# First two chunks of a linear-attention and gated-FFN block: one group of weight maxima less, a weight cast shared by two engines, other small moves, and the last output in two parts

## The chip, the cores and the metric

One core of one Trainium2 chip. The metric is the device time of one execution in microseconds (us); of several executions the median is given. TensorE is called PE (its weight loads PEld), VectorE DVE, ScalarE ACT, GpSimd POOL and SyncE SP. PEq, DVEq, ACTq, POOLq and SPq are the queues from which an engine issues register loads and DMAs.

## The reference

The input x is 8 x 1024 tokens of 256 channels, in float32. With xn = layernorm(x) the output is x + attention(xn) + ffn(xn):

```
q = elu(xn @ Wq.T) + 1;  k = elu(xn @ Wk.T) + 1;  v = xn @ Wv.T         (16 heads of 16)
attn = (q @ (k.T v)) / max(q @ sum(k), 1e-6)                           (per head, over 1024 tokens)
local = xn[t-1]*conv_w[:,0] + xn[t]*conv_w[:,1] + xn[t+1]*conv_w[:,2] + conv_b
attention = (attn + local) @ Wp.T + bp
ffn = (silu(xn @ wg.T) * (xn @ wu.T)) @ wd.T                           (768 hidden, int32 weights / 127)
```

## The kernel before

The kernel works through 16 chunks of 512 tokens, two (c = 0, 1) to each of the 8 batches b. Weights are brought in once. To multiply in float16 without losing float32's precision, each operand is the sum of a high part (suffix `h`) and a low part (`l`), and a product takes three matmuls (high x high, low x high, high x low). The integer weights of gate, up and down (g, u, d) need no low part if they are small; a flag that is read into a register (`TENSOR_LOAD`, then a branch) tells that. A power of two that scales a weight into float16's range comes from the maximum of that weight over all its elements.

Such a maximum is made in stages. DVE reduces each weight along its rows (`weight_maximum`, L665). For a **group** of weights (`GROUPS`) PE transposes the column of maxima (`turn_maxima`, L1056), DVE takes the maximum of each row (L647) and puts it on a diagonal (L649, together `across`), PE multiplies by ones so that every partition has it (`spread_maxima`, L1063), and DVE makes the powers and scales of it (`powers`, L656 to L661, four short steps, each waiting for the one before). The groups are [k, v, q], [g, u], [d] and [conv_w, conv_b, p], numbered 0 to 3. Group 3 gives the scales of the convolution's taps (`attention_scales`), group 2 that of d (`down_scales`).

A chunk's step on PE is: k and v (`project_kv(0)`, `(1)`), q, accumulation of k.T v, six blocks of gate and up (`gate_up(0)` to `(5)`, 8 matmuls of 512 columns each), and the down projection in two halves (`down(0)`, `down(1)`, 24 matmuls of 256 columns each). `gate_up(j)` from j = 2 on waits for `hid` of block j - 2, since it takes that block's PSUM banks. On ACT a block is silu (`act_g`, L536) and the high part of the hidden values (`hh`, L544); on DVE it is the product (`hid`, L896) and the low part (`hl`, L902). `down(0)` waits for `hid` of block 4, then for each `hh` and `hl`.

Every engine has a program written out by hand: its `step` function lists the work in the order in which the engine does it, and semaphores hold engines together. Nothing is reordered at run time, so an instruction that waits holds all that stand behind it on its engine. The first chunk (`not past`) is special: the scales are made in between, and k and v of this chunk are multiplied in float32 straight from the raw weights (`project_first`, L1085). In the second chunk (b = 0, c = 1) the float16 weights of k and v are used for the first time: `project_kv` waits for `k_hi`, `v_hi` and, at its last third, for `kv_lo` (both low parts, `kv_wl`, L677). Chunks from b = 1 on attend to the batch before as well.

What the prediction's steps touch in the first chunk:

- DVE: v's high part (L709), `gate_up_scales`, g's high part (L684), the statistics of the next chunk's layernorm (`stats`), d's maximum, then `hid` and `hl` mixed with `across(2)`, `down_scales` and the late maxima of p, conv_w and conv_b; at its end `across(3)`, `attention_scales` (with `cb`, L764, and `cw`, L768), the two `kv_wl` and the two residual sums (`put_res`, L912).
- ACT: u's high part (`u_wh`, L455), table load, silu and `hh` of each block, the next chunk's `xn_h` (`x_high`, L444), d's high part (`d_wh`, L455) behind silu of block 3, and q's exponential at the end.
- POOL: k's high part (L393), k's sum (`k_sb`, L397), the normalised tokens (L326), their low part (`xn_l`, L408), the issue of two DMAs that add x to the bias in `xb` (L323), the transposed tokens `xT` (L361), and q's sum (`q_sb`, L416).
- SP: all other loads, the two transposing DMAs of `xn_h` and `xn_l`, and the stores.

At the end DVE writes the last 256 tokens of the output in one instruction (`output`, L823) and SP stores them in one DMA (`store_pair`).

## Time and profile before

| | |
|---|---|
| median of 3 runs | 507.55 us (507.19 to 507.74) |
| profiled execution, its own time | 506.9 us |
| its span in the profile | 505.3 us |
| PE busy | 491.4 us, 97% |
| PEld busy | 306.1 us, 61% |
| DVE busy | 430.5 us, 85% |
| ACT busy | 334.3 us, 66% |
| POOL busy | 144.7 us, 29% |
| chain that ended last | PE 88%, DVE 5%, ACT 3%, DMA 2% |
| granted PE clock | 0.999 of full speed |

The time is some 1.6 us longer than the span, which begins and ends with the first and last recorded instruction. The profiled execution lies 0.65 us below the median. The page's slices (12.6 us each) show PE at 7, 8, 8, 8 tenths in the first four slices, at 9 in all others but the last, which is at 7. A timeline row gives the start in us, the duration in us, engine, line and operation, output and inputs, and in square brackets the idle time before it and what ended it; several like instructions in a row share one line, whose duration runs from the first start to the last end.

### The profile page before, as it was taken

How to read it: one execution, taken by the hardware profiler on the slowest of the kernel's cores; microseconds unless marked ns; L12 is line 12 of the kernel's file. 1: busy time of each engine (PE TensorE's matmuls, PEld its weight loads, DVE VectorE, ACT ScalarE, POOL GpSimd, SP SyncE). 2: the span in 40 equal slices, each digit the busy share in tenths (PEclk: the TensorE clock that was granted, in tenths of full speed). 3: DMA queues.
4: the chain of work that ended last, by engine and by line, in shares of the span. 5: the costliest groups of instructions: out<-in, count | busy, mean ns of one | idle time of the engine just before them, and what ended most of it. 6: DMA issues, size and time to landing. Idle time of an engine off the chain costs nothing.

```text
span 505.3 us, 11017 instructions
## 1 busy us (share of the span) xinstructions
PE 491.4 (97%) x3968; PEld 306.1 (61%) x3968; DVE 430.5 (85%) x833; ACT 334.3 (66%) x522; POOL 144.7 (29%) x152
## 2 busy tenths in 40 slices
PE   7888999999999999999999999999999999999997
PEld 6545364755747566474756657475565756657576
DVE  4889898889888898988889888889888889897786
ACT  2676866667485775757667485667758576674770
...
DMA packets 68653, 45.36 MB, mean 90 GB/s; under 512 B 33424, under 2 KB 68112, under 8 KB 68624
## 3 DMA queue, kind: packets, MB, share of 16 engines
...
q14 instruction: 10, 0.08, 0.0%
...
## 4 chain that ended last, share of the span: by engine, by line
PE 88%; DVE 5%; ACT 3%; DMA 2%; issue 1%; ACTq 0%; DVEq 0%
PE ps L1202 16%; PE ps L1039 16%; PE ps L1211 15%; PE ps L1221 15%; PE ps L1145 15%; PE ps L1101 5%; PE ps L1110 3%; PE ps L1164 2%; DMA wv_raw<-in_L_attn_Wv_dram 2%; DVE maxima L665 1%; DVE hl L902 1%; DVE hid L896 1%; ACT hh L544 1%; DVE cb L764 0%; PE ps L1085 0%
## 5 line engine op out<-in xcount | busy, mean ns | idle before, releaser
L536 ACT ACTIVATE act_g<-ps,scales 128x512 f32<-128x512 f32 x96 | 65.9, 687 | 42.0 <-PE ps L1211 39.7
L896 DVE SCALAR_TENSOR_TENSOR hid<-act_g,scales,ps 128x512 f32<-128x512 f32 x96 | 71.4, 744 | 21.2 <-ACT act_g L536 20.7
L902 DVE TENSOR_TENSOR hl<-hid,hh 128x512 f16<-128x512 f32 x96 | 66.3, 691 | 1.8 <-ACT hh L544 0.4
L361 POOL TENSOR_TENSOR xT<-xh,xl 128x1024 f32<-128x1024 f16 x15 | 32.3, 2153 | 109.4 <-issue 109.4
L544 ACT ACTIVATE hh<-hid 128x512 f16<-128x512 f32 x96 | 59.7, 622 | 5.3 <-DVE hid L896 5.3
L1202 PE MATMUL ps<-xh,g_wh 128*128 128x512 f16 x192 | 57.6, 382 | 2.1 <-ACT u_wh L455 1.4
L1211 PE MATMUL ps<-xl,g_wh 128*128 128x512 f16 x192 | 57.1, 379 | 0.0
L1202 PE MATMUL ps<-xh,u_wh 128*128 128x512 f16 x192 | 57.1, 379 | 0.0
L1211 PE MATMUL ps<-xl,u_wh 128*128 128x512 f16 x192 | 57.1, 379 | 0.0
L1221 PE MATMUL ps<-d_wh,hh 128*128 128x256 f16 x384 | 52.4, 273 | 2.2 <-DVE hid L896 2.2
L499 ACT ACTIVATE k_neg<-ps,scales 128x512 f32<-128x512 f32 x30 | 20.6, 687 | 49.4 <-PE ps L1145 49.4
L1221 PE MATMUL ps<-d_wh,hl 128*128 128x256 f16 x384 | 52.7, 273 | 0.1
L326 POOL TENSOR_SCALAR xn<-x_in,neg_mean,rstd 128x256 f32<-128x256 f32 x62 | 51.5, 843 | 4.3 <-POOL rstd L333 4.2
L473 ACT ACTIVATE local<-xT,cb,cw 128x512 f32<-128x512 f32 x32 | 24.3, 807 | 42.3 <-POOL xT L361 39.3
L832 DVE SCALAR_TENSOR_TENSOR local<-xT,cw,local 128x512 f32<-128x512 f32 x60 | 45.2, 790 | 0.4 <-ACT local L473 0.4
L1221 PEld LDWEIGHTS ps<-d_wh,hh 128*128 128x128 f16 x384 | 37.3, 98 | 7.5 <-ACT hh L544 2.2
L1221 PEld LDWEIGHTS ps<-d_wh,hl 128*128 128x128 f16 x384 | 37.3, 98 | 5.1 <-DVE hl L902 0.7
L912 DVE SCALAR_TENSOR_TENSOR res<-ps,scales,xb 128x512 f32<-128x512 f32 x32 | 23.7, 746 | 17.3 <-PE ps L1221 17.3
L357 POOL TENSOR_TENSOR xT<-xh,xl 128x2 f32<-128x2 f16 x8 | 1.8, 224 | 122.2 <-DMA xl<-xn_l 85.8
L333 POOL TENSOR_TENSOR rstd<-var_eps,half 128x4 f32<-128x4 f32 x15 | 15.9, 1057 | 72.6 <-DVE var_eps L622 72.6
L1101 PEld LDWEIGHTS ps<-state,q_sb 128*128 128x128 f32 x256 | 32.1, 190 | 2.9 <-DVE hid L896 0.6
L1101 PE MATMUL ps<-state,q_sb 128*128 128x136 f32 x256 | 32.5, 279 | 0.3 <-DVE hid L896 0.3
...
## 6 DMA issues: line engine op xcount, KB each, us to landing
xb<-bp_sb SPq DMA_DIRECT2D x16, 512.0 KB, 3.4
xb<-in_L_attn_x_dram POOLq DMA_DIRECT2D x16, 512.0 KB, 5.9
x_in<-in_L_attn_x_dram SPq DMA_DIRECT2D x15, 512.0 KB, 4.1
out_dram<-out_sb SPq DMA_DIRECT2D x14, 512.0 KB, 2.9
out_dram<-out_sb SPq DMA_DIRECT2D x4, 256.0 KB, 2.1
...
```

The source lines that it names most:

```text
L326: return nc.gpsimd.tensor_scalar(xn[:, i, :], x_in[:, c, i, :], neg_mean[:, c, i:i + 1], rstd[:, c, i:i + 1], ALU.add, ALU.mult)
L536: nc.scalar.activation(act_g[:, j % 2, :], ps[:, gate_bank(j), :], ACT.Silu, scale=silu_in).then_inc(silu_ready, 1)
L544: nc.scalar.activation(hh[:, j, :], hid[:, j % 2, :], ACT.Copy).then_inc(hh_ready, 1)
L832: nc.vector.scalar_tensor_tensor(out=here, in0=xT[:, c, k, side:side + CHUNK], scalar=cw[:, k, side:side + 1], in1=here, op0=ALU.mult, op1 ...
L896: nc.vector.scalar_tensor_tensor(out=hid[:, j % 2, :], in0=act_g[:, j % 2, :], scalar=h_mul, in1=ps[:, gate_bank(j) + 1, :], op0=ALU.mult, ...
L902: nc.vector.tensor_tensor(hl[:, j, :], hid[:, j % 2, :], hh[:, j, :], ALU.subtract).then_inc(hl_ready, 1)
L1039: ins = nc.tensor.matmul(dst, stat(s, k), mov(m, k), start=(n == 0 and k == 0), stop=(n == len(TERMS) - 1 and k == KT - 1))
L1101: ins = nc.tensor.matmul(ps[:, banks[p] + i % 2, k * AW:(k + 1) * AW], q_sb[:, c, k, i * P:(i + 1) * P], state[:, k, :], start=True, stop= ...
L1145: ins = nc.tensor.matmul(ps[:, 2 * p + i, :], x2[s][:, c, 2 * p + i, k, :], kv_w[m][:, k, :], start=(n == 0 and k == 0), stop=(n == len(TE ...
L1202: nc.tensor.matmul(dst, w[0][:, k, cols], xh[:, c, :, k, :], start=(k == 0), stop=False)
L1211: ins = nc.tensor.matmul(tiles_of(gate_bank(j) + n), w[0][:, k, j * P:(j + 1) * P], xl[:, c, :, k, :], start=False, stop=(k == KT - 1))
L1221: ins = nc.tensor.matmul(ps[:, banks[p], i * D:(i + 1) * D], h[:, j, t], w[:, j, :], start=start and i == 0, stop=stop, skip_group_check=True)
```

## The change

1. **Groups.** p's, conv_w's and conv_b's maxima join d's in group 2; group 3 is gone, and with it one `turn_maxima`, one `across`, one `spread_maxima` and one `powers`. DVE takes the late maxima behind `hid` of block 0, and `across(2)` comes behind `hl` of block 0. Group 1 uses another PSUM bank (6), and its transpose no longer waits for group 0's scales.
2. **u_wh and d_wh by two engines each.** DVE makes the second half of `u_wh` (768 of 1536 columns) behind `g_wh`; ACT makes the first. POOL makes the last third of `d_wh` (512 of 1536 columns), behind `xn_l` and ahead of the two `xb` DMAs; ACT makes the rest.
3. **v's high part** goes from DVE to ACT, behind silu of block 0.
4. **Flags.** PE reads the flag for gate and up before it waits for their weights, and the flag for down before `gate_up(5)` instead of behind it.
5. **Group 1's spread** stands on PE between k and v of the last 128 tokens, not behind both.
6. **attention_scales** has six steps ahead of `cb` and `cw` no more, but five, and none of the former `powers(3)`; `cb` is a tensor_tensor with a broadcast scale, `cw` a scalar_tensor_tensor.
7. **Second chunk.** q's relu on DVE comes ahead of two taps. POOL, not DVE, makes `xn_l` of the third chunk, and DVE makes p's low part (`p_wl`) in that place instead of behind the state.
8. **Last output** in two instructions of 256 columns; SP stores the first, ACT's queue the second.

```diff
-        GROUPS = [["k", "v", "q"], ["g", "u"], ["d"], ["cw", "cb", "p"]]
+        GROUPS = [["k", "v", "q"], ["g", "u"], ["d", "cw", "cb", "p"]]
...
-        MAX_BANK = [7, 7, 7, STATE]
+        MAX_BANK = [7, STATE, 7]
...
+            sp.wait_ge(out_ready, NB * CB * 2)
+            sp.dma_start(out_v[NB * CB - 1][:, 2, :], out_sb[:, 1, 2, :]).then_inc(out_stored[1], 16)
...
-                    if isinstance(b, int) and b == 0 and c == 0:
+                    if isinstance(b, int) and b == 0:
+                        if c == 1:
+                            pool.wait_ge(xl_turned, 16)
                         for p in range(2):
-                            pool.wait_ge(xn_h_ready, p + 1)
+                            pool.wait_ge(xn_h_ready, 2 * c + p + 1)
                             tiles = slice(2 * p, 2 * p + 2)
                             nc.gpsimd.tensor_tensor(xn_l[:, tiles, :], xn[:, tiles, :], xn_h[:, tiles, :],
                                                     ALU.subtract).then_inc(xn_l_ready, 1)
+                    if isinstance(b, int) and b == 0 and c == 0:
+                        pool.wait_ge(scaled[2], 1)
+                        pool.sem_inc(norms_due, 1)
+                        nc.gpsimd.tensor_scalar(d_w[0][:, D_BY_ACT:J, :],
+                                                ffn_raw["d"][:, D_BY_ACT * D:J * D].rearrange("p (k n) -> p k n", n=D),
+                                                col(scale_up, "d"), None, ALU.mult).then_inc(d_hi, 1)
                         add_x(0, 0)
...
-                    high(u_w[0][:, :, :], ffn_raw["u"][:, :].rearrange("p (k n) -> p k n", k=KT), "u", gate_up_hi)
+                    high(u_w[0][:, 0, :], ffn_raw["u"][:, 0:HID], "u", gate_up_hi)
...
+                    if j == 0 and not past:
+                        high(kv_w[0][:, :, D:2 * D], w_raw["v"][:, :, :], "v", v_hi)
...
-                        high(d_w[0][:, :, :], ffn_raw["d"][:, :].rearrange("p (k n) -> p k n", k=J), "d", d_hi)
+                        high(d_w[0][:, 0:D_BY_ACT, :],
+                             ffn_raw["d"][:, 0:D_BY_ACT * D].rearrange("p (k n) -> p k n", n=D), "d", d_hi)
...
+            act.wait_ge(out_ready, NB * CB * 2 + 1)
+            act.dma_start(out_v[NB * CB - 1][:, 3, :], out_sb[:, 1, 3, :]).then_inc(out_stored[1], 16)
...
-                powers(3)
-
-                scale_op(nc.vector.tensor_scalar(part_a, col(power, "v"), 512.0, None, ALU.mult))
-                scale_op(nc.vector.scalar_tensor_tensor(out=part_b, in0=col(power, "cw"), scalar=128.0, in1=part_a,
-                                                        op0=ALU.mult, op1=ALU.add))
...
-                nc.vector.tensor_scalar(cb[:, :], cb_raw[:, :], y_up, None, ALU.mult).then_inc(taps_made, 1)
+                scale_op(nc.vector.tensor_scalar(y_up, part_c, W_UP / 2, None, ALU.mult))
+                nc.vector.tensor_tensor(cb[:, :], cb_raw[:, :], y_up.broadcast_to([P, KT]), ALU.mult).then_inc(taps_made, 1)
+                nc.vector.scalar_tensor_tensor(out=cw[:, :, :], in0=cw_raw[:, :, :], scalar=1.0 / X_UP,
+                                               in1=y_up.unsqueeze(2).broadcast_to([P, KT, 3]), op0=ALU.mult,
+                                               op1=ALU.mult).then_inc(taps_made, 1)
...
-                    gate_up_high("g", g_w)
+                    gate_up_high("g", g_w[0][:, :, :], ffn_blocks("g", KT))
+                    gate_up_high("u", u_w[0][:, 1, :], ffn_raw["u"][:, HID:2 * HID])
                     stats(nb, ncx)
                     weight_maximum("d")
                     gate_up_low_halves()
                     hidden(0)
+                    late_maxima()
+                    hidden(1)
+                    hidden_low(0)
                     across(2)
                     put_state()
-                    hidden(1)
-                    hidden_low(0)
                     hidden(2)
+                    hidden_low(1)
                     down_scales()
-                    hidden_low(1)
                     hidden(3)
                     hidden_low(2)
-                    late_maxima()
...
-                    across(3)
                     attention_scales()
...
-                if g == len(GROUPS) - 1:
-                    pe.wait_ge(acc_kept, 1)
-                elif g > 0:
-                    pe.wait_ge(scaled[g - 1], 1)
+                if g == 2:
+                    pe.wait_ge(scaled[0], 1)
...
                     gate_up(1)
+                    gate_up(2)
                     turn_maxima(2)
-                    gate_up(2)
+                    gate_up(3)
                     spread_maxima(2)
-                    gate_up(3)
                     gate_up(4)
-                    gate_up(5)
-                    turn_maxima(3)
-                    pe.wait_ge(hid_ready, J - 1)
-                    pe.wait_ge(d_hi, 1)
                     pe.wait_ge(down_seen, 1)
                     is_wide["down"] = pe.value_load(wide[0:1, 2:3].bitcast(I32))
+                    gate_up(5)
+                    pe.wait_ge(hid_ready, J - 1)
+                    pe.wait_ge(d_hi, 2)
                     down(0, DOWN)
-                    spread_maxima(3)
                     down(1, DOWN)
```

In the listings of program order below, the line numbers of the change's rows are those of its own code, some 10 to 20 lines further down. PE of the first chunk around group 1's spread, before (L1085 is `project_first`, L1056 and L1063 the maxima's transpose and spread, L1039 q's matmuls):

```order
L1085 MATMUL ps<-wv_raw,xT 128x256 x2
L1056 MATMUL ps<-ident,maxima 2x128
L1085 MATMUL ps<-wk_raw,xT 128x256 x2
L1085 MATMUL ps<-wv_raw,xT 128x256 x2
L1063 MATMUL ps<-spread,ones 128x2
L1039 MATMUL ps<-xh,q_wh 128x512 x2
```

The same place in the change:

```order
L1103 MATMUL ps<-wv_raw,xT 128x256 x2
L1075 MATMUL ps<-ident,maxima 2x128
L1103 MATMUL ps<-wk_raw,xT 128x256 x2
L1082 MATMUL ps<-spread,ones 128x2
L1103 MATMUL ps<-wv_raw,xT 128x256 x2
L1060 MATMUL ps<-xh,q_wh 128x512 x2
```

The spread has moved ahead of the last pair of v's matmuls; nothing else here has.

DVE of the first chunk from `hid` of block 0 on, before (L647 and L649 are `across(2)`, L873 the kept accumulation, L656 the first step of `down_scales`):

```order
L896 SCALAR_TENSOR_TENSOR hid<-act_g,scales,ps 128x512
L647 TENSOR_REDUCE group_max<-ps 1x1
L649 TENSOR_SCALAR spread<-ident,group_max 1x1
L873 COPY first_acc<-ps 128x66
L896 SCALAR_TENSOR_TENSOR hid<-act_g,scales,ps 128x512
L902 TENSOR_TENSOR hl<-hid,hh 128x512
L896 SCALAR_TENSOR_TENSOR hid<-act_g,scales,ps 128x512
L656 TENSOR_SCALAR over_all<-ps 128x1
```

The same place in the change (L680 are the maxima of p, conv_w and conv_b):

```order
L917 SCALAR_TENSOR_TENSOR hid<-act_g,scales,ps 128x512
L680 TENSOR_REDUCE maxima<-wp_raw 128x1
L680 TENSOR_REDUCE maxima<-cw_raw 128x1
L680 TENSOR_REDUCE maxima<-cb_raw 128x1
L917 SCALAR_TENSOR_TENSOR hid<-act_g,scales,ps 128x512
L923 TENSOR_TENSOR hl<-hid,hh 128x512
L662 TENSOR_REDUCE group_max<-ps 4x1
L664 TENSOR_SCALAR spread<-ident,group_max 4x4
L894 COPY first_acc<-ps 128x66
L917 SCALAR_TENSOR_TENSOR hid<-act_g,scales,ps 128x512
L923 TENSOR_TENSOR hl<-hid,hh 128x512
L671 TENSOR_SCALAR over_all<-ps 128x4
```

`across(2)` now stands behind `hid` of block 1 and `hl` of block 0 and ahead of `hid` of block 2, and it works on four rows and columns, not one.

PE from the last matmuls of `gate_up(5)` to the start of `down(1)`, before (L1275 reads the flag for down, L1221 are down's matmuls, those between the two L1240 are skipped):

```order
L1211 MATMUL ps<-xl,u_wh 128x512 x2
L1056 MATMUL ps<-ident,maxima 3x128
L1275 TENSOR_LOAD wide
L1221 MATMUL ps<-d_wh,hh 128x256 x10
L1221 MATMUL ps<-d_wh,hl 128x256 x8
L1221 MATMUL ps<-d_wh,hh 128x256 x2
L1240 COMPARE_AND_BRANCH
L1221 MATMUL ps<-d_wl,hh 128x256 x12
L1240 UNCONDITIONAL_BRANCH
L1221 MATMUL ps<-d_wh,hl 128x256 x4
L1063 MATMUL ps<-spread,ones 128x3
L1221 MATMUL ps<-d_wh,hh 128x256 x10
```

In the change, from the last matmuls of `gate_up(4)` to the start of `down(0)`:

```order
L1229 MATMUL ps<-xl,u_wh 128x512 x2
L1293 TENSOR_LOAD wide
L1220 MATMUL ps<-xh,g_wh 128x512 x2
L1220 MATMUL ps<-xh,u_wh 128x512 x2
L1221 COMPARE_AND_BRANCH
L1225 MATMUL ps<-xh,g_wl 128x512 x2
L1225 MATMUL ps<-xh,u_wl 128x512 x2
L1221 UNCONDITIONAL_BRANCH
L1229 MATMUL ps<-xl,g_wh 128x512 x2
L1229 MATMUL ps<-xl,u_wh 128x512 x2
L1239 MATMUL ps<-d_wh,hh 128x256 x10
```

The flag's load stands ahead of `gate_up(5)`; the transpose ahead of `down(0)` and the spread between `down(0)` and `down(1)` are gone.

## Rows read from the trace of the kernel before

**Rows 1.** A window: length; PE, PEld, DVE, ACT, POOL busy; clock, DMA share, GB/s.

```profile
72.00:100.00 28.00, 28.00 (x231) 17.07 (x230) 25.61 (x49) 18.99 (x31) 7.55 (x9) 1.00 0.35 77
```

**Rows 2.** Timeline, PE in the first two chunks.

```profile
16.66 0.27 PE L1056 MATMUL ps<-ident,maxima 128*2 128x128 f32 x1 [0.50 <-DVE scales L690]
...
23.17 0.59 PE L1202 MATMUL ps<-xh,g_wh 128*128 128x512 f16 x2 [1.42 <-ACT u_wh L455]
...
33.53 0.61 PE L1202 MATMUL ps<-xh,g_wh 128*128 128x512 f16 x2 [0.24 <-DVE hid L896]
...
37.13 1.25 PE L1221 MATMUL ps<-d_wh,hh 128*128 128x256 f16 x10 [1.59 <-DVE hid L896]
...
40.84 1.27 PE L1221 MATMUL ps<-d_wh,hh 128*128 128x256 f16 x10
...
46.54 1.04 PE L1145 MATMUL ps<-kv_wl,xh 128*128 128x512 f16 x4 [1.18 <-DVE kv_wl L677]
```

**Rows 3.** Timeline, DVE in the first chunk.

```profile
19.29 0.59 DVE L658 TENSOR_SCALAR power<-over_all 128x2 int32<-128x2 int32 x1
...
20.72 1.01 DVE L684 TENSOR_SCALAR g_wh<-wg_int,scale_up 128x1536 f16<-128x1536 int32 x1
...
23.97 1.75 DVE L665 TENSOR_REDUCE maxima<-wd_int 128x1 f32<-128x1536 int32 x1
...
30.84 0.15 DVE L656 TENSOR_SCALAR over_all<-ps 128x1 f32<-128x1 f32 x1
...
31.87 0.15 DVE L740 TENSOR_TENSOR scales<-scales,power 128x1 f32<-128x1 f32 x1
```

**Rows 4.** Timeline, ACT in the first chunk.

```profile
20.99 1.59 ACT L455 ACTIVATE u_wh<-wu_int,scale_up 128x1536 f16<-128x1536 int32 x1
...
26.54 0.63 ACT L444 ACTIVATE xn_h<-xn 128x512 f16<-128x512 f32 x1 [0.76 <-POOL xn L326]
...
32.70 1.56 ACT L455 ACTIVATE d_wh<-wd_int,scale_up 128x1536 f16<-128x1536 int32 x1
```

**Rows 5.** Timeline, POOL and DVE where both worked.

```profile
18.59 1.26 POOL L397 TENSOR_TENSOR k_sb<-k_exp,k_relu 128x512 f32<-128x512 f32 x1 [0.30 <-ACT k_exp L516]
...
29.42 1.28 POOL L408 TENSOR_TENSOR xn_l<-xn,xn_h 128x512 f16<-128x512 f32 x1 [0.73 <-ACT xn_h L444]
...
37.85 2.60 POOL L361 TENSOR_TENSOR xT<-xh,xl 128x1024 f32<-128x1024 f16 x1
...
39.01 1.46 DVE L649 TENSOR_SCALAR spread<-ident,group_max 3x3 f32<-3x3 f32 x1
...
42.41 2.34 POOL L416 TENSOR_TENSOR q_sb<-q_exp,q_relu 128x1024 f32<-128x1024 f32 x1 [1.95 <-ACT q_relu L585]
...
42.91 1.86 DVE L764 TENSOR_SCALAR cb<-cb_raw,scales 128x2 f32<-128x2 f32 x1
...
68.63 2.27 DVE L880 TENSOR_TENSOR state<-whole_acc,head_mask 128x256 f32<-128x256 f32 x1
```

**Rows 6.** Timeline, DVE's low parts of v and of the third chunk's tokens.

```profile
45.73 0.75 DVE L677 SCALAR_TENSOR_TENSOR kv_wl<-wv_raw,scale_up,kv_wh 128x512 f16<-128x512 f32 x1
...
63.68 1.28 DVE L632 TENSOR_TENSOR xn_l<-xn,xn_h 128x512 f16<-128x512 f32 x2
```

**Rows 7.** Groups of the page's part 5, of a block's hidden values: busy, mean ns.

```profile
L896 DVE SCALAR_TENSOR_TENSOR hid<-act_g,scales,ps 128x512 f32<-128x512 f32 x96 | 71.4, 744 | 21.2 <-ACT act_g L536 20.7
L902 DVE TENSOR_TENSOR hl<-hid,hh 128x512 f16<-128x512 f32 x96 | 66.3, 691 | 1.8 <-ACT hh L544 0.4
```

**Rows 8.** The issue of two sums into xb, and DMA issues up to 60 us.

```profile
30.65 2.84 POOL L323 DMA_DIRECT2D xb<-in_L_attn_x_dram  x2
...
xb<-in_L_attn_x_dram POOLq DMA_DIRECT2D x3, 512.0 KB, 7.3
```

**Rows 9.** The page's DMA issues of the output (KB each, us to landing).

```profile
out_dram<-out_sb SPq DMA_DIRECT2D x14, 512.0 KB, 2.9
out_dram<-out_sb SPq DMA_DIRECT2D x4, 256.0 KB, 2.1
```

More of the change, by code:

```diff
@@ L98, in build @@
         gate_up_wide = sb("gate_up_wide", [P, 1])
-        scales = sb("scales", [P, 15])
+        scales = sb("scales", [P, 14])
         def col(of, name):
@@ L105, in group @@
             return of[:, COL[GROUPS[g][0]]:COL[GROUPS[g][-1]] + 1]
-        (q_down, k_down, q_flip, k_flip, y_up, tap_up, attn_to_y, y_down, silu_in, h_mul, f_down,
-         part_a, part_b, part_c, part_d) = (scales[:, i:i + 1] for i in range(15))
+        (q_down, k_down, q_flip, k_flip, y_up, attn_to_y, y_down, silu_in, h_mul, f_down,
+         part_a, part_b, part_c, part_d) = (scales[:, i:i + 1] for i in range(14))
         x_in = sb("x_in", [P, CB, TILES, D])
@@ L825, in output, with last_output @@
                                                op0=ALU.mult, op1=ALU.add).then_inc(out_ready, 1)
+            def last_output(banks):
+                dve.wait_ge(wp_done, NB * CB * 2)
+                dve.wait_ge(res_ready, NB * CB * 2)
+                dve.wait_ge(out_stored[1], (NB - 1) * 16)
+                for i in range(2):
+                    nc.vector.scalar_tensor_tensor(out=out_sb[:, 1, 2 + i, :], in0=ps[:, banks[1], i * D:(i + 1) * D],
+                                                   scalar=y_down, in1=res[:, 1, 2 + i, :],
+                                                   op0=ALU.mult, op1=ALU.add).then_inc(out_ready, 1)
             def tap(b, c, k, side):
@@ L974, in step @@
                             y_low(b - 1, c, 1)
-                        if j == (X_SPLIT if attend else FIRST_X_SPLIT):
+                        if j == FIRST_X_SPLIT and not attend:
+                            low(p_w[1][:, :, :], w_raw["p"][:, :, :], "p", p_w[0][:, :, :], p_hi, 1, p_lo)
+                        if j == X_SPLIT and attend:
                             x_low(nb, ncx, 0)
@@ L984, in step @@
                         output(b - 1, c, 1, WP)
-                    if not attend:
-                        low(p_w[1][:, :, :], w_raw["p"][:, :, :], "p", p_w[0][:, :, :], p_hi, 1, p_lo)
                     put_res(0, DOWN)
@@ L1022, in step @@
                     output(b, 1, 0, LAST_WP[1])
[L1023 removed]
+                    last_output(LAST_WP[1])
             run(dve, step)
@@ L1076, in turn_first, with project_first @@
                 ins.then_inc(first_turned, 1)
[L1078 removed]
+            def project_first(p, i, n):
                 pe.wait_ge(first_xT, p + 1)
[L1081 to L1087 removed]
+                pe.wait_ge(w_in[n], 16)
+                t, half = 2 * p + i, "kv".index(n)
+                for k in range(KT):
+                    ins = nc.tensor.matmul(ps[:, t, half * D:(half + 1) * D], xT[:, 0, k, 1 + t * P:1 + (t + 1) * P],
+                                           w_raw[n][:, k, :], start=(k == 0), stop=(k == KT - 1))
+                if (i, n) == (1, "v"):
                     ins.then_inc(kv_done, 1)
```

59 lines of the change are left out of this document (25 added, 34 removed).

## The prediction

> **What bounds the kernel now.** I read the windows first: in the loop over chunks PE is busy 28.00 of 28 us, DVE 25.61 and ACT 18.99 [rows 1]. There PE's own work is the time, and no edit touches it. So a shift of PE's start into the loop carries through to the end one for one. What can be won is PE's idle time in the first two chunks, and the tail. Next the timeline of PE: ahead of its rows stand gaps of 0.50, 1.42, 0.24, 1.59 and 1.18 us [rows 2]; with a wait ahead of the spread between down(0) and down(1), which shows as 3.71 us from start to start where 24 matmuls need about 2.6, they come to some 6 us. In this stretch the kernel is bound by chains through DVE and ACT, so I follow those chains with the durations of their rows, to the last gap, the wait of the second chunk for `kv_wl` at 46.54.
>
> **The change, part by part.**
>
> *Group 1 and the gate/up weights.* Group 1's transpose drops its wait: PE's 0.50 us at 16.66 goes [rows 2]. Its spread is one pair of matmuls earlier, and v's high part is off DVE, so `powers(1)` starts behind `q_wl` at some 18.1. Its steps are some 0.17 us apart (seven from 30.84 to 32.02 in `down_scales`, the first and the last in rows 3). Before, its second step took 0.59 us instead of some 0.17 and ended with POOL's `k_sb` (18.59 to 19.85) [rows 3, 5]: a DVE operation with both sides in SBUF sat out POOL's instruction. The last steps or `g_wh` itself now fall into the same `k_sb`, so `g_wh` starts no sooner than 19.9 (20.4 if several steps are still to come), against 20.72 [rows 3]. I take 19.9. Behind it DVE makes half of `u_wh`: half of 1.01 us and a fixed part, 0.6 us. ACT's half costs 0.9 of its 1.59 us [rows 4] and ends near 21.8. PE has read the flag by then, so gate_up(0) starts at 21.8 to 22.0, against 23.17: 1.3 us won here.
>
> *This gain is lost again.* DVE stands 0.8 - 0.6 = 0.2 us better behind `u_wh` than before. The statistics and d's maximum (23.97 to 25.72 before [rows 3]) end at 25.5, `hid` 0 at 26.4, the late maxima (p's third of the columns of d's 1.75 us [rows 3], 0.6, and two small ones: 0.85 in all) at 27.2. They fill a wait for silu, since `xn_h` comes 0.2 us earlier than 26.54 [rows 4] and silu of block 1 stands behind it on ACT: `hid` 1 runs 27.6 to 28.3. v's high part on ACT lies ahead of `xn_h` in idle time (0.76 us of it in rows 4, more ahead of silu 0), so I cost it at nothing; without that cover it would cost 0.7. Then `hl` 0 (0.69 us, as `hid` takes 0.74 [rows 7]; silu and `hh` on ACT I take at 0.7 and 0.6, since they also pass over 512 columns), `across(2)`. Its diagonal is now 4x4; a 3x3 one took 1.46 us while POOL ran `xT`, and ended as `xT` did [rows 5]. POOL's second `xn_l` (1.28 us, [rows 5]) is free to start when `hl` 0 ends, at 29.1, and would hold the diagonal to 30.4. The bounds are 0.2 us (not held) and 1.3; I take the hold, as the 3x3 row is its nearest. `hid` 2 then ends at 31.4, `hl` 1 at 32.1, `down_scales` (30.84 to 32.02 before, 1.2 us [rows 3]) at 33.3, `hid` 3 at 34.05. gate_up(5) waits for it and starts at 34.1, against 33.53 [rows 2]: 0.6 us *later*. The flag for down is read by PE from 33.2 on; no row shows such a load alone. It lies within the 1.59 us gap at 37.13, so its cost is between 0 and 1.5 us; at up to 0.9 it hides behind `hid` 3, and I take that.
>
> *Down.* `d_wh` on ACT is two thirds of 1.56 us [rows 4], 1.1, from 33.3 to 34.4; POOL's third, by the same share and twice as slow, takes 0.5 to 1.6 us and is there by 34.9. Silu 4 and `hid` 4 end at 35.85. down(0) starts then, against 37.13, since the flag's load and the transpose no longer stand in front of it. Its last matmuls wait for `hl` 5 (silu 5, `hid` 5, `hh` 5, `hl` 5 in a row), at 38.8. down(1) follows directly at 39.1, against 40.84 [rows 2]: 1.7 us. Between down(1) and the wait for `kv_wl` lie 46.54 - 40.84 - 1.18 = 4.5 us of work, so PE arrives at 43.6.
>
> *The taps' scales.* DVE is through `hl` 5 at 38.8. Ahead of `cb` are 5 short steps (1.2 us with the branch), where before came `across(3)`, `powers(3)` and 6. `cb` took 1.86 us and ended with POOL's `q_sb` [rows 5]. Now POOL is in `xT` (2.60 us at 37.85 before; later by the `d_wh` share and two issues of 2.84 us that stand behind it [rows 8], hidden before by a wait for the transposing DMAs) to about 40.7; `cb`, `cw` and `attn_to_y` end at 41.1, and two `kv_wl` of 0.75 us [rows 6] at 42.6, 1.0 us ahead of PE. The 1.18 us gap is gone: 46.54 becomes 43.6, **2.9 us won**.
>
> *Second chunk.* q's relu ahead of two taps ends a short wait of gate_up(1), but gate_up(2) waits for `hid` 0, whose silu ACT sets: nothing. DVE's `xn_l` (1.28 us) is replaced by `p_wl` (0.74) [rows 6]: up to 0.5 us won ahead of down(0); POOL's two `xn_l` can hold DVE's `hl`, which reads two tensors in SBUF: up to 1.2 us lost each. I take 0, with -0.5 and +2.4 as ends.
>
> *Tail.* The last output waits for PE as before. Two halves end a little later than one whole, since each has its own fixed part (0.1 us by g's and u's share above); the last DMA is 128 KB instead of 256. From 512 to 256 KB landing falls from 2.9 to 2.1 us [rows 9]; half of that once more, 0.4, is the upper end, 0 the lower. I take 0.3 won net.
>
> Sum: 2.9 + 0 + 0.3 = 3.2 us on the profiled execution, 506.9 us, 503.7 then. The median was 0.65 us above it: 507.55 - 3.2 = **504.3 us**. About 0.2%, 1.0 us, is what a measurement of this kernel can tell from no change.
>
> **The rivals.**
>
> *A. The diagonal is not held* (POOL's `xn_l` is over or not begun). For it: the two start within some tenths of each other, and rows of `across` that meet nobody would be short; against it: the times above. `hid` 2 comes 1.1 us earlier and the blocks stay ahead to the end: 503.2 us, with half of the second chunk's 0.5 us 503.0.
>
> *B. POOL's hold falls on the low parts.* `kv_wl` of v is behind `q_sb` (2.34 us [rows 5]) if ACT's q chain ends a little sooner than 42.6 or DVE's steps a little later; the margin is a few tenths. Then it ends near 45.7, PE waits 2.1 us, and 0.8 of the 2.9 are left: 506.4 at worst, 505.5 if only a part is held. For it: `state`, two inputs in SBUF, took 2.27 us beside `xT`, whose start was 0.13 us sooner [rows 5]. The Trainium skill (SBUF — State Buffer, Who interferes with whom) says that a DVE instruction with two SBUF inputs contends with a GpSimd one that reads SBUF, and that whoever issues first has the shared ports for its whole instruction. By that rule the new forms of `cb` and `cw` are held just as the old one; the trace agrees with it in the row of `state`.
>
> *C. No change.* `res` of the first chunk needs the sum in `xb`, whose DMA is issued 3.6 us later than at 30.65, behind `scaled[2]` and `d_wh`; landing takes 7.3 us in the median [rows 8]. At 34.3 + 7.3 = 41.6 it is in time; PE needs `res` at about 44.5. A landing some 5 us slower gives the gain back: 507.
>
> *D. Slower.* POOL holds DVE at every new meeting: `q_sb` on `kv_wl` (2.1 us of PE), both `xn_l` on `hl` in the second chunk (2.4 us), and `hid` 2 as in the forecast. 504.3 + 2.1 + 2.4 = 508.8. It decides against the change once holds on the path exceed 4.2 us beyond the forecast's. Against it: at each meeting POOL must be the one that starts first, and `hl` at 0.69 us in the mean of 96 [rows 7] is hardly ever held now.
>
> **How the numbers follow.** Forecast (503.6 to 505.1) 0.45, A 0.2, B 0.2, C 0.08, D 0.07. The forecast, A and nearly all of B are faster by over 1.0 us: 0.85; same 0.08, slower 0.07. The range takes in A's best and most of B: 502.6 to 505.9.
>
> **What would show it.** Right: gate_up(0) near 21.9, no gap ahead of down(0) but that for `hid` 4, down(1) straight behind down(0), `kv_wl` ready before PE, the first `kv_wl` matmul 2.9 us earlier. Step "lost again" is wrong if gate_up(5) starts before 33.5; then A. B shows as a `kv_wl` of over 1 us, C as a wait of DVE's `res` for a DMA. In the second chunk, `hl` over 1 us beside POOL's `xn_l`. Wrong altogether if PE enters the loop no earlier, or if it idles within it.

## The result: slightly slower, not 3.2 us faster

| | before | after |
|---|---|---|
| median of 21 runs | 507.36 us (506.85 to 508.29) | 508.89 us (506.94 to 510.75) |
| profiled execution, its span | 506.9, 505.3 us | 509.02, 507.4 us |
| PE, DVE, POOL busy | 491.4, 430.5, 144.7 us | 493.4, 430.8, 148.5 us |

The ratio is 1.0027, 95% interval [1.0018, 1.0037]: slower by 0.9 to 1.9 us, where 504.3 us was forecast.

First the windows: the end of `down(0)` and most of `down(1)` of the first chunk, and the loop (columns as in [rows 1]).

```profile
40.00:41.00 1.00, 0.39 (x2) 0.11 (x2) 1.00 (x2) 0.97 (x2) 0.00 (x0) 0.97 1.11 158
41.00:44.00 3.00, 2.84 (x14) 2.04 (x15) 2.83 (x11) 2.77 (x4) 1.61 (x1) 0.50 0.73 117
...
72.00:100.00 28.00, 27.22 (x221) 15.98 (x219) 23.28 (x45) 19.60 (x32) 8.50 (x7) 1.00 0.39 83
```

Two things are new. From 41 to 44 PE has half its clock (0.50: 1.2 of 2.4 GHz), and from 72 to 100 it is no longer busy for the whole of the 28 us. The timeline of PE, against [rows 2]:

```profile
22.46 0.60 PE L1220 MATMUL ps<-xh,g_wh 128*128 128x512 f16 x2 [0.66 <-ACT u_wh L465]
...
33.66 0.60 PE L1220 MATMUL ps<-xh,g_wh 128*128 128x512 f16 x2 [0.51 <-DVE hid L917]
...
35.55 1.05 PE L1239 MATMUL ps<-d_wh,hh 128*128 128x256 f16 x8
...
40.56 0.39 PE L1239 MATMUL ps<-d_wh,hl 128*128 128x256 f16 x2 [2.21 <-DVE hl L923]
41.16 0.61 PE L1239 MATMUL ps<-d_wh,hl 128*128 128x256 f16 x2 [0.21 <-DVE hl L923]
41.56 2.34 PE L1239 MATMUL ps<-d_wh,hh 128*128 128x256 f16 x10
...
45.55 1.03 PE L1163 MATMUL ps<-kv_wh,xh 128*128 128x512 f16 x4
...
47.27 1.03 PE L1163 MATMUL ps<-kv_wl,xh 128*128 128x512 f16 x4
```

Up to `down(0)` the time comes out as forecast: it starts at 35.55 (35.85 forecast, 37.13 before). Then PE stands idle for 2.21 us within `down(0)`, waiting for a low part `hl`, and the ten matmuls that open `down(1)` take 2.34 us where they took 1.27 [rows 2]. The 1.6 us won have become 0.7 us lost at 41.56, then 2.1 us at the first `kv_wh` matmul (45.55 for 43.47), and 0.73 us at the first `kv_wl` matmul (47.27 for 46.54), since before waited there for `kv_wl` (1.18 us [rows 2]) and after does not. POOL and DVE in that stretch, against [rows 5]:

```profile
28.99 1.41 POOL L412 TENSOR_TENSOR xn_l<-xn,xn_h 128x512 f16<-128x512 f32 x1 [0.16 <-ACT xn_h L454]
...
29.61 0.81 DVE L664 TENSOR_SCALAR spread<-ident,group_max 4x4 f32<-4x4 f32 x1
...
34.67 2.83 POOL L325 DMA_DIRECT2D xb<-in_L_attn_x_dram  x2
...
36.47 1.26 POOL L359 TENSOR_TENSOR xT<-xh,xl 128x2 f32<-128x2 f16 x1
...
36.77 3.17 POOL L363 TENSOR_TENSOR xT<-xh,xl 128x1024 f32<-128x1024 f16 x1
...
36.99 4.11 DVE L923 TENSOR_TENSOR hl<-hid,hh 128x512 f16<-128x512 f32 x2
...
41.97 0.16 DVE L774 TENSOR_TENSOR cb<-cb_raw,scales 128x2 f32<-128x2 f32 x1
...
42.20 0.74 DVE L692 SCALAR_TENSOR_TENSOR kv_wl<-wk_raw,scale_up,kv_wh 128x512 f16<-128x512 f32 x1
...
42.39 2.75 POOL L426 TENSOR_TENSOR q_sb<-q_exp,q_relu 128x1024 f32<-128x1024 f32 x1 [2.45 <-ACT q_relu L598]
...
42.86 2.83 DVE L692 SCALAR_TENSOR_TENSOR kv_wl<-wv_raw,scale_up,kv_wh 128x512 f16<-128x512 f32 x1
```

POOL's three `xT` instructions start at 36.47, ahead of `hl` of blocks 4 and 5 at 36.99. The two small ones take 1.26 and 1.25 us and end at 37.73 and 37.87, just behind the issue of the two sums into `xb`, which runs to 37.50; where they start a microsecond behind that issue, as in experiment 1 (38.47), they take 0.2. The large one ends at 39.94. The two `hl`, which need 1.47 us elsewhere, take 4.11 and end at 41.10. `cb`, on which the forecast put the meeting with `xT`, is free at 0.16. `q_sb` meets `kv_wl` of v, as in rival B, but PE is too late to feel it.

The later losses, by PE's, DVE's, POOL's and SP's timelines of the second and third chunk (PE was at 65.68 and 82.89 before in the places of the rows at 66.77 and 85.20):

```profile
64.16 2.91 POOL L412 TENSOR_TENSOR xn_l<-xn,xn_h 128x512 f16<-128x512 f32 x2 [9.03 <-ACT xn_h L454]
...
64.41 1.65 DVE L692 SCALAR_TENSOR_TENSOR p_wl<-wp_raw,scale_up,p_wh 128x512 f16<-128x512 f32 x1
...
66.77 1.27 PE L1239 MATMUL ps<-d_wh,hh 128*128 128x256 f16 x10 [0.92 <-DVE hid L917]
...
67.02 1.34 POOL L325 DMA_DIRECT2D xb<-in_L_attn_x_dram  x1
...
67.16 1.23 SPq L254 DMA_TRANSPOSE xl<-xn_l  x1
...
72.89 2.12 POOL L363 TENSOR_TENSOR xT<-xh,xl 128x1024 f32<-128x1024 f16 x1 [4.52 <-issue]
...
84.81 0.46 PE L1182 MATMUL ps<-v_sb,k_sb 128*32 128x33 f32 x32 [0.59 <-DVE k_sb L869]
```

From +0.73 us at the first `kv_wl` matmul the lag grows to +0.92 at the second chunk's gate_up(0), +1.09 at its down(0), and +2.31 at the third chunk's gate_up(0) (85.20 for 82.89). It stays there to the last output (504.21 for 501.90). `p_wl` takes 1.65 us beside POOL's `xn_l`. `xT` of the third chunk is 4.4 us later than at 68.50, since its transposing DMA is issued 1.9 us later, right behind the sum into `xb`, and takes 2.5 us longer. The DMA issues from 66 to 75 us in after:

```profile
xb<-in_L_attn_x_dram POOLq DMA_DIRECT2D x1, 512.0 KB, 7.4
...
xl<-xn_l SPq DMA_TRANSPOSE x1, 5.6
```

and the same DMA in before, 64 to 72 us:

```profile
xl<-xn_l SPq DMA_TRANSPOSE x1, 3.1
```

This row of the page answers to [rows 7]; the mean of `hl` grew from 691 to 726 ns.

```profile
L923 DVE TENSOR_TENSOR hl<-hid,hh 128x512 f16<-128x512 f32 x96 | 69.7, 726 | 1.7 <-ACT hh L554 0.4
```

**How often the clock falls.** Each run lists its mean granted clock. In before it was 0.999 or 1.000 in the profiled run and in every comparison run of the experiments. In after it was 0.996 or 0.997 in 16 of 21 runs (median 508.97 us), and 0.999 or 1.000 in the other five (median 507.74). So the fall is not certain, and by these medians it costs some 1.2 us in after when it comes.

### The profile page after: what moved, and what is told of

Same layout as the page of the kernel before. It is cut to its first block, busy times and chain, and to the rows that moved or that the text cites. A ratio compares the mean times of both kernels' runs of the same rounds, so it can differ in the third digit from the quotient of the medians.

```text
span 507.4 us, 11010 instructions
## 1 busy us (share of the span) xinstructions
PE 493.4 (97%) x3965; PEld 306.7 (60%) x3965; DVE 430.8 (85%) x824; ACT 333.7 (66%) x523; POOL 148.5 (29%) x155
## 3 DMA queue, kind: packets, MB, share of 16 engines
HBM read 20.32 MB, written 8.39 MB: 57 GB/s over the span
## 4 chain that ended last, share of the span: by engine, by line
PE 81%; DVE 2%; issue 2%; ACT 1%; POOL 1%; DVEq 0%
PE ps L1060 15%; PE ps L1220 15%; PE ps L1229 14%; PE ps L1239 14%; PE ps L1163 13%; PE ps L1119 5%; PE ps L1128 3%; PE ps L1182 2%; DVE local L853 1%; ACT local L483 0%; POOL xT L363 0%; DVE y L817 0%; DVE bn_raw L620 0%; DVE hl L923 0%; POOL xb L325 0%
## 5 line engine op out<-in xcount | busy, mean ns | idle before, releaser
L923 DVE TENSOR_TENSOR hl<-hid,hh 128x512 f16<-128x512 f32 x96 | 69.7, 726 | 1.7 <-ACT hh L554 0.4
L1239 PE MATMUL ps<-d_wh,hh 128*128 128x256 f16 x384 | 53.7, 277 | 1.5 <-DVE hid L917 0.9
```

The source lines that it names most:

```text
L923: nc.vector.tensor_tensor(hl[:, j, :], hid[:, j % 2, :], hh[:, j, :], ALU.subtract).then_inc(hl_ready, 1)
L1239: ins = nc.tensor.matmul(ps[:, banks[p], i * D:(i + 1) * D], h[:, j, t], w[:, j, :], start=start and i == 0, stop=stop, skip_group_check=True)
```

## The experiments

Each ran 5, 11 or 12 times (last column) beside the kernel before, whose median there was 507.34 us (experiments 1 to 4), 507.18 (5 to 8) and 507.02 (9 to 11); the ratios go by these. The start of a run jitters by up to 1 us: PE's first product of k began between 9.96 and 11.10 in the profiles, 10.08 in both before and after. This table gives, for the profiled run of each kernel, times from that product, the common start, to four starts on PE; the last column counts the runs at a mean clock of 0.997 or less. The common start does not take all of the jitter out: with the same code up to there, gate_up(0) of the first chunk comes between 11.66 us (experiments 4 and 6) and 12.59 us (experiment 7) behind it. So a difference of under half a microsecond between two rows says little.

| kernel | ch. 2 `kv_wl` | ch. 2 gate_up(0) | ch. 2 down(0) | ch. 3 gate_up(0) | median us | ratio to before | clock fell |
|---|---|---|---|---|---|---|---|
| before | 36.46 | 43.62 | 55.60 | 72.81 | 507.36 | | |
| after | 37.19 | 44.54 | 56.69 | 75.12 | 508.89 | 1.0027 [1.0018, 1.0037] | 16 of 21 |
| xT behind hl | 35.26 | 42.42 | 54.76 | 72.69 | 507.34 | 1.0008 [0.9995, 1.0021] | 3 of 12 |
| xn_l on DVE | 36.79 | 44.15 | 55.93 | 73.14 | 507.59 | 0.9997 [0.9985, 1.0009] | 9 of 12 |
| both | 35.62 | 42.78 | 54.76 | 71.97 | 506.70 | 0.9988 [0.9973, 1.0003] | 6 of 12 |
| PE kept busy | 35.38 | 42.55 | 54.89 | 73.06 | 507.24 | 1.0002 [0.9994, 1.0011] | 0 of 12 |
| all holds away | 33.18 | 40.85 | 52.33 | 69.54 | 504.39 | 0.9947 [0.9934, 0.9961] | 0 of 5 |
| low parts first | 32.69 | 40.73 | 52.16 | 69.37 | 504.54 | 0.9947 [0.9934, 0.9961] | 0 of 5 |
| xb sum early | 36.44 | 43.60 | 55.94 | 73.46 | 507.68 | 1.0016 [1.0004, 1.0027] | 7 of 11 |
| tail alone | 36.45 | 43.61 | 55.60 | 72.81 | 506.82 | 0.9995 [0.9986, 1.0004] | 0 of 11 |
| xn_l left on POOL | 33.17 | 40.83 | 52.68 | 71.15 | 505.04 | 0.9961 [0.9947, 0.9974] | 0 of 5 |
| casts by one engine | 33.44 | 40.62 | 52.57 | 69.78 | 504.00 | 0.9936 [0.9922, 0.9950] | 0 of 5 |
| diagonal not held | 33.87 | 41.54 | 53.02 | 70.23 | 503.45 | 0.9928 [0.9914, 0.9942] | 0 of 5 |

**1. `xT` behind `hl`.** After, and POOL's `xT` of the second chunk waits for all six `hl`.

```diff
                     pool.wait_ge(first_xl, 1)
+                    if c == 1:
+                        pool.wait_ge(hl_ready, J)
```

> The changed kernel, with POOL's xT of the second chunk made to wait for the last hl of the first. Theory P (the shared ports in the first chunk: hl is held by xT for 3.4 us, PE idles 2.2 us and then gets half its clock for 3 us): hl of block 4 takes 0.7 us, PE waits under 0.5 us ahead of it, the granted clock is 1.00 throughout, PE's first matmul on kv_wl comes 2.5 to 3.5 us sooner than 47.3 unless kv_wl is then held by xT or q_sb, and the time is 505.5 to 506.8. Theory S (the loss is made in the second and third chunk, by xn_l on POOL and the late transposing DMA): the time stays at 508 or above. Theory G (the gaps won are given back to whatever comes next): PE reaches kv_wl sooner and waits there; the time is 507 to 508.

Timelines of DVE, POOL and PE:

```profile
36.82 1.47 DVE L925 TENSOR_TENSOR hl<-hid,hh 128x512 f16<-128x512 f32 x2
...
38.78 2.12 POOL L365 TENSOR_TENSOR xT<-xh,xl 128x1024 f32<-128x1024 f16 x1
...
39.12 1.80 DVE L768 SCALAR_TENSOR_TENSOR scales<-power 128x1 f32<-128x1 f32 x1 [0.82 <-issue]
...
42.23 2.65 POOL L428 TENSOR_TENSOR q_sb<-q_exp,q_relu 128x1024 f32<-128x1024 f32 x1 [1.33 <-ACT q_relu L600]
...
42.60 2.83 DVE L694 SCALAR_TENSOR_TENSOR kv_wl<-wv_raw,scale_up,kv_wh 128x512 f16<-128x512 f32 x1
...
45.49 1.04 PE L1165 MATMUL ps<-kv_wl,xh 128*128 128x512 f16 x4 [2.40 <-DVE kv_wl L694]
```

The two `hl` are back at 1.47 us and the wait within `down(0)` is gone: `xT` was what held them. At the second chunk's first `kv_wh` matmul 4.5 us are won against after from the common start (30.97 for 35.47), but at `kv_wl` only 1.9 (35.26 for 37.19): PE now waits 2.40 us for `kv_wl` of v, which `q_sb` holds. Rival B was right about that place; another loss in front of it hid it in after. The time, 507.34 us, lies above the 505.5 to 506.8 of theory P and in the range of theory G.

**2. `xn_l` on DVE.** After, with the second chunk's order of before: the third chunk's `xn_l` on DVE, `p_wl` at the end, and the `xb` sum early.

```diff
-                    if isinstance(b, int) and b == 0:
-                        if c == 1:
-                            pool.wait_ge(xl_turned, 16)
+                    if isinstance(b, int) and b == 0 and c == 0:
...
-                        if j == FIRST_X_SPLIT and not attend:
-                            low(p_w[1][:, :, :], w_raw["p"][:, :, :], "p", p_w[0][:, :, :], p_hi, 1, p_lo)
-                        if j == X_SPLIT and attend:
+                        if j == (X_SPLIT if attend else FIRST_X_SPLIT):
                             x_low(nb, ncx, 0)
...
```

> The changed kernel, with the third chunk's xn_l back on DVE and p's low part back at the end of the second chunk, so that POOL's sum into xb is also issued early again. Theory S: the transposing DMA of xl lands in 3.1 us instead of 5.6, ACT's first tap of the third chunk no longer waits for xT, PE's 0.8 us of waits for k_sb there are gone, and the time is 1.0 to 1.6 us less than the changed kernel's, 507.3 to 507.9. Theory P alone: within 0.3 us of the changed kernel, 508.9.

From the first `kv_wl` matmul to the third chunk's gate_up(0) PE takes 36.35 us (73.14 - 36.79), as in before (36.35); in after 37.93. The DMA lands in 3.1 us again. This part of the change costs 1.6 us in the profiles; the medians (507.59 for 508.89) say 1.3.

**3. Both.** Edits 1 and 2 together.

> Both edits of the two runs before. If both losses are real and independent, the two gains add up: 504.0 to 505.5, faster than the kernel before by 0.4 to 0.6%. If one hides behind the other: no better than the better of the two alone.

506.70 us, so the two gains do not add up to the 504.0 to 505.5 expected. PE still waits 2.41 us for `kv_wl`, and the six runs with the lower clock have a median of 507.91, the other six of 505.46. That wait is the only one of over 1.0 us that PE's timeline shows behind 12 us; that the clock falls behind it is likely, but not shown, since the profiled run kept its clock. The same holds of experiment 1, with 509.36 us in three runs and 507.00 in nine. By such medians the fall costs some 2.4 us in these two, 2.0 in experiment 2, 1.2 in after and 1.0 in experiment 7; why it differs stays open.

**4. PE kept busy.** After, and eight matmuls of 128 columns into an unused bank ahead of the last low-part matmuls of `down(0)`. Nothing of the result depends on them.

```diff
+                    if not past and p == 0:
+                        pe.wait_ge(acc_kept, 1)
+                        for _ in range(8):
+                            nc.tensor.matmul(ps[:, STATE, 0:P], ident[:, :], ident[:, :], start=True, stop=True)
```

> The changed kernel, with 8 matmuls of 128 columns into an unused PSUM bank ahead of the last four low-part matmuls of down(0), where PE idles for 2.2 us. They compute nothing that is used. If the half clock from 41 to 44.4 us follows from that idle time, the granted clock is 1.00 and the time is 1.2 to 1.6 us less, 507.3 to 507.7, with hl held as before. If the clock falls for another reason, or its loss is hidden by a later wait (kv_wl is held until 45.7), the time stays within 0.4 us of 508.9.

PE's timeline, with the fillers (x16, since a float32 matmul is recorded twice) in place of the idle stretch:

```profile
38.01 1.95 PE L1265 MATMUL ps<-ident 128*128 128x128 f32 x16
40.39 0.39 PE L1239 MATMUL ps<-d_wh,hl 128*128 128x256 f16 x2 [0.43 <-DVE hl L923]
...
41.22 1.25 PE L1239 MATMUL ps<-d_wh,hh 128*128 128x256 f16 x10
...
43.84 1.03 PE L1163 MATMUL ps<-kv_wh,xh 128*128 128x512 f16 x4
```

`hl` is held as before (4.12 us), but `down(1)` takes 2.62 us (41.22 to 43.84) where it took 3.99 (41.56 to 45.55), and none of 12 runs has the lower clock. So in the profiled runs the fall costs 1.37 us, and it does not come where PE is kept busy. By the median 1.65 us come back.

**5. All holds away.** Edits 1 and 2, and POOL's `q_sb` waits for both `kv_wl`.

```diff
                     pool.wait_ge(q_read, 1)
+                    pool.wait_ge(kv_lo, 2)
                     nc.gpsimd.tensor_tensor(q_sb[:, 0, :, :], q_exp[:, :, :], q_relu[:, :, :],
```

> The third run's kernel (xT behind the last hl, xn_l of the third chunk on DVE), and POOL's q_sb of the first chunk made to wait for both kv_wl. Theory G, as the first three runs leave it: kv_wl of v, held by q_sb for 2.1 us, is the next thing that PE waits for (2.4 us), and nothing is behind it. Then that wait falls to 0.0 to 0.5 us, kv_wl of v takes 0.75 us, and the time is 1.9 to 2.6 us less than the 506.7 of the third run: 504.0 to 504.9. Rival R (something else in the second chunk sets its pace, as the xT or q_sb that is now late, or ACT's q chain): less than 1 us is won, 505.7 to 506.7.

```profile
42.34 0.74 DVE L693 SCALAR_TENSOR_TENSOR kv_wl<-wv_raw,scale_up,kv_wh 128x512 f16<-128x512 f32 x1
...
43.14 1.04 PE L1164 MATMUL ps<-kv_wl,xh 128*128 128x512 f16 x4 [0.32 <-DVE kv_wl L693]
...
43.26 2.35 POOL L427 TENSOR_TENSOR q_sb<-q_exp,q_relu 128x1024 f32<-128x1024 f32 x1 [2.62 <-DVE kv_wl L693]
```

504.39 us, faster than both kernels. The first `kv_wl` matmul starts 3.28 us earlier than in before from the common start, and the lead is 3.27 us at the third chunk's gate_up(0). It is the forecast's first chunk, reached by two waits that the change did not have. Not every hold is gone: `xT` now meets the first step of the taps' scales, which takes 1.72 us (38.94 to 40.66), and PE waits 0.32 us for `kv_wl`.

**6. Low parts first.** Edit 2, both `kv_wl` ahead of `attention_scales` on DVE, `xT` behind `kv_wl`, and `q_sb` behind the taps (`taps_made`).

> xn_l of the third chunk on DVE; DVE makes both kv_wl ahead of the scales of the taps, xT waits for both kv_wl and q_sb for cb and cw. PE never waits for kv_wl. If the taps and k's parts on ACT have slack, 503.8 to 504.9, no slower than the run before it. If ACT's taps (which need xT) are then on the path, k_neg of the second chunk starts 1 to 1.5 us behind its matmuls, and the time is 0.5 to 1.5 us more than the run before it.

```profile
41.90 2.12 POOL L365 TENSOR_TENSOR xT<-xh,xl 128x1024 f32<-128x1024 f16 x1
...
42.29 1.75 DVE L775 TENSOR_TENSOR cb<-cb_raw,scales 128x2 f32<-128x2 f32 x1
```

504.54 us: a different order that keeps `hl` and `kv_wl` clear of POOL gives the same time. `cb` in its new form is held like the old one was (1.86 us [rows 5]).

**7. xb sum early.** After, with the third chunk's sum into `xb` issued ahead of POOL's `xn_l`, as in before, and `xn_l` left on POOL.

```diff
                         if c == 1:
+                            add_x(nb, ncx)
                             pool.wait_ge(xl_turned, 16)
```

> The changed kernel, with the third chunk's sum into xb issued ahead of POOL's xn_l and not behind it. If the transposing DMA of xl is slow because this sum runs beside it (5.6 us to landing against 3.1), it lands in 3.0 to 3.6 us again, and 1 us or less of the third chunk's loss goes: 507.9 to 508.6. If it is slow by itself, or late only since POOL is slower than DVE at xn_l, landing stays over 5 us and the time at 508.9.

DMA issues from 62 to 74 us:

```profile
xl<-xn_l SPq DMA_TRANSPOSE x1, 3.0
```

Timelines of DVE, POOL and PE in the first chunk:

```profile
20.93 1.70 DVE L701 TENSOR_SCALAR u_wh<-wu_int,scale_up 128x768 f16<-128x768 int32 x1
...
20.95 1.26 POOL L399 TENSOR_TENSOR k_sb<-k_exp,k_relu 128x512 f32<-128x512 f32 x1 [1.08 <-ACT k_exp L528]
...
41.32 0.39 PE L1241 MATMUL ps<-d_wh,hl 128*128 128x256 f16 x2 [2.21 <-DVE hl L925]
...
42.15 1.26 PE L1241 MATMUL ps<-d_wh,hh 128*128 128x256 f16 x10
```

The DMA is back from 5.6 to 3.0 us, and from the first `kv_wl` matmul to the third chunk's gate_up(0) PE takes 37.02 us: 0.9 of the 1.6 us of experiment 2 come back. By difference, the other 0.7 is the meeting of `p_wl` and `xn_l` and its delay of DVE. The median is 507.68, a little under the 507.9 to 508.6 expected. This profiled run kept its clock: its `down(1)` takes 2.62 us (42.15 to 44.77) though PE was idle for 2.21 us ahead of it. It also shows a meeting that the forecast did not list: DVE's half of `u_wh` with POOL's second `k_sb`. Here `u_wh` takes 1.70 us, and PE waits 1.59 us for it ahead of gate_up(0); in after `u_wh` starts 0.42 us before `k_sb` and takes 0.61.

**8. Tail alone.** Before, with the last output in two parts.

> The kernel before, with nothing but the last output in two parts. The sum had 0.3 us for it: 507.0 against 507.3, at the edge of what five rounds tell. The time from the last matmul's start to the end of the span falls from 3.8 us to 3.4 to 3.7 us. If the second queue's DMA starts late or costs more, it is no shorter.

```profile
501.81 0.88 DVE L836 SCALAR_TENSOR_TENSOR out_sb<-ps,scales,res 128x256 f32<-128x256 f32 x2 [0.56 <-PE ps L1052]
```

From the start of PE's last matmuls to the span's end 3.6 us remain (501.39 to 505.0) for 3.8 (501.48 to 505.3). The interval takes in 1; by the profile 0.2 us.

**9. `xn_l` left on POOL.** Experiment 5 without edit 2.

> The changed kernel with POOL's transposed-x copies of the second chunk behind all of hl, and its q_sb of the first chunk behind both kv_wl; the third chunk's xn_l and p_wl stay where the change put them. So it is the run with all holds away (504.39 us) less one of its parts: the low part of the third chunk on POOL. My theory, each hold is a loss of its own and the third chunk's late transposing DMA costs 0.5 to 1.3 us: 505.0 to 505.7, POOL's xT of the third chunk at 69 to 70 with its transposing DMA in flight over 4.5 us, and PE waiting on k_sb of that chunk for 0.3 to 0.8 in all. Rival: the second and third chunk's order costs nothing once the first chunk is in time, since the time that PE would wait is covered: 504.2 to 504.6, without such a wait.

PE's timeline in the third chunk:

```profile
80.77 0.46 PE L1185 MATMUL ps<-v_sb,k_sb 128*32 128x33 f32 x32 [0.79 <-DVE k_sb L872]
```

The third chunk's transposing DMA takes 5.4 us, and `k_sb` comes late by 0.79 us. 505.04 us, 0.65 above experiment 5 by the medians (the intervals of the ratios overlap) and 1.6 at the third chunk's gate_up(0) by the profiles (71.15 for 69.54). The second half of the change's loss is there with or without the first.

**10. Casts by one engine.** Experiment 5 with `u_wh` and `d_wh` made by ACT alone. With POOL's part of `d_wh` its wait for group 2's scales goes too, so the two sums into `xb` are issued earlier (30.92).

```diff
-D_BY_ACT = 4
+D_BY_ACT = 6
...
-                    high(u_w[0][:, 0, :], ffn_raw["u"][:, 0:HID], "u", gate_up_hi)
+                    high(u_w[0][:, :, :], ffn_raw["u"][:, :].rearrange("p (k n) -> p k n", k=KT), "u", gate_up_hi)
...
-                    gate_up_high("u", u_w[0][:, 1, :], ffn_raw["u"][:, HID:2 * HID])
```

> The run with all holds away (504.39 us), with its split of u_wh and d_wh over two engines undone: both are made by ACT alone, as before the change. Theory of the prediction, what is won ahead of gate/up(0) is lost again by gate/up(5), since the hidden values are then the limit: gate/up(0) 0.4 to 0.6 us later, gate/up(5) and down(0) within 0.3 us of that run, d_wh 1.1 us longer on ACT beside gate/up(4) but hidden, total 504.2 to 505.0. Rival: the split is worth what it saves ahead of gate/up(0) and d_wh holds up the silu of block 4, so that down(0) begins 0.8 us or more later: 505.2 to 506.0.

PE's timeline (its first product of k is 0.75 us later than in experiment 5):

```profile
23.42 0.60 PE L1215 MATMUL ps<-xh,g_wh 128*128 128x512 f16 x2 [1.30 <-ACT u_wh L461]
...
34.43 0.60 PE L1215 MATMUL ps<-xh,g_wh 128*128 128x512 f16 x2 [0.69 <-DVE hid L913]
...
36.73 1.28 PE L1234 MATMUL ps<-d_wh,hh 128*128 128x256 f16 x10 [0.41 <-DVE hid L913]
```

From the common start gate_up(0) is 0.65 us later (12.71 for 12.06), gate_up(5) 0.45 (23.72 for 23.27), down(0) 0.86 (26.02 for 25.16), but the `kv_wl` matmul only 0.26. `down(0)` was expected within 0.3 us of experiment 5. The median is 504.00, below experiment 5's 504.39. In the profiles the two split casts bring 0.65 us ahead of gate_up(0) and 0.24 us at the third chunk's gate_up(0); in the medians they bring nothing.

**11. Diagonal not held.** Experiment 5, and POOL's second `xn_l` waits for the spread of group 2 (`max_spread[2]`).

> The run with all holds away (504.39 us), and POOL's second xn_l of the second chunk also waits for the spread of group 2's maxima, so that no POOL instruction with two inputs from SBUF runs while DVE puts the maxima on the diagonal (0.81 us there, held). Theory: the 0.6 us of that hold stand in front of the powers, of down_scales and of hid 3, on which gate/up(5) waits, so gate/up(5) begins 0.3 to 0.6 us earlier, and the time is 503.8 to 504.1. Rival: hid 3 is set by silu and by the low parts ahead of it, or the POOL instruction now falls on another two-input one of DVE; then gate/up(5) is where it was and the time is 504.3 to 504.6, or up to 1 us more if xT comes late enough to hold up k and v of the second chunk.

```profile
30.22 0.22 DVE L667 TENSOR_SCALAR spread<-ident,group_max 4x4 f32<-4x4 f32 x1
...
30.59 1.15 POOL L414 TENSOR_TENSOR xn_l<-xn,xn_h 128x512 f16<-128x512 f32 x1 [1.14 <-DVE spread L667]
...
31.15 1.14 DVE L926 TENSOR_TENSOR hl<-hid,hh 128x512 f16<-128x512 f32 x1
```

The diagonal falls from 0.81 to 0.22 us, and `hl` 1 rises from 0.67 to 1.14: the hold has moved to the next DVE instruction with two inputs in SBUF. Of the 0.59 us won on the diagonal 0.47 are lost on `hl` 1: from `hid` 0 to `hid` 3, on which gate_up(5) waits, DVE takes 6.98 us (26.37 to 33.35) for 7.12 in experiment 5 (25.32 to 32.44), where 0.3 to 0.6 less was expected. The median, 503.45 us, is the lowest of all, and the two ratios' intervals (0.9914 to 0.9942 against 0.9934 to 0.9961) just overlap; but the profiled run shows a gain of 0.14 us and not of 0.9, so where the rest would come from, if it is real, stays open.

## Why the prediction was wrong

*Group 1 and the gate/up weights*: right in kind, half in size. `g_wh` started at 20.32, between the 19.9 that the sum took and its 20.4, and gate_up(0) at 22.46, where 21.8 to 22.0 was forecast: 0.7 us won for 1.3. The `k_sb` hold fell on the flag's step (`wide`, 0.99 us).

*This gain is lost again*: right in kind. gate_up(5) came at 33.66, 0.1 later than before, where 0.6 was forecast; the diagonal was held to 30.42, as forecast (30.4). So 0.8 us were lost between the two, and 1.9 were forecast. That `down(0)` came within 0.3 us of its forecast is luck in part: the gain was overrated, and so was its loss. In experiment 10 such a gain is lost only in part: 0.65 us at gate_up(0), 0.45 at gate_up(5), 0.26 at `kv_wl`.

*Down*: **this is the step that failed**, with *the taps' scales*. It has `hl` 5 done at 38.8 and PE going on with `down(1)` at 39.1; `hl` 5 was done at 41.10 and `down(1)` began at 41.56. In the same sum, `xT` (2.60 us) ends at 40.7, so it runs from 38.1, across `hl` 5 (38.1 to 38.8). The rule of POOL's hold was put on `cb` behind it and never on `hl`, though `hl` reads two tensors in SBUF; the second chunk's part even says so. Rival D lists holds on `kv_wl`, on the second chunk's `hl` and on `hid` 2, but not this one. Besides, `xT` was "later by the `d_wh` share and two issues" to 38.1; its three instructions began at 36.47 to 36.77. The transposing DMA that they wait for took 4.8 us where it took 6.3 in before. The likely reason is that the two sums are issued 4 us later (34.67 for 30.65 [rows 8]) and run beside its end only; with experiment 10's earlier sums (30.92) it took 5.7. So `hl` 4 was caught as well as `hl` 5, for 2.21 us of PE's time. Experiment 1 takes it away.

*What the idle time did*: no step had it. In before PE waits 1.59 us at most in this stretch [rows 2]; the 2.21 us wait is followed by half the clock in most executions, worth 1.37 us (experiment 4). Without it, as experiment 4 has it, after would be level with before (507.24 us).

*The taps' scales*: the forecast's 43.6 for the first `kv_wl` matmul was the right time for a first chunk without holds (43.14 in experiment 5). In the change as made, rival B's hold of `kv_wl` by `q_sb` lay underneath: 2.40 us of PE in experiment 1, near the 2.1 of B's full price.

*Second chunk*: taken at 0, between -0.5 and +2.4; it was +1.6 us (0.9 by the late DMA and `xT`, 0.7 by `xn_l`; experiments 2 and 7). The sum counted POOL's instruction, but not that POOL's `xb` DMA stood behind it and would run beside the transposition for the third chunk. *Tail*: 0.2 us for 0.3. Rival C was not seen: `res` of the first chunk did not wait for its DMA. Its sum is short, too: 41.6 and 5 us more are 2.1 us beyond 44.5, and that takes back 2.1 of the 3.2 us, not all.

From the common start, after's first `kv_wl` matmul lies 4.01 us behind experiment 5's, and the third chunk's gate_up(0) 5.58: the 3.3 us to be won, and the 2.3 lost on top. Rival D had the sign and nearly the time (508.8), by POOL's holds at new meetings, but for the most part with other meetings, and without the clock and the late DMA; that its number fits is luck.

The Trainium skill (SBUF — State Buffer, Who interferes with whom) says that issue order, not the shape of the operation, decides who blocks. The trace agrees, by the recorded starts: `xT` (36.77) ahead of `hl` (36.99) in after, `q_sb` (42.39) ahead of `kv_wl` of v (42.86), and in experiment 5, with the starts turned round, `kv_wl` takes 0.74 us. Where the recorded starts lie 0.02 us apart, they do not tell who is held: in experiment 7 `u_wh` (20.93) is held by `k_sb` (20.95), while in experiment 4, with 21.05 and 21.07, `u_wh` takes 0.61 us and `k_sb` 1.72.
